# Edge loop of a graph transformer on one core: sums added plainly from a slot read from a table

## The reference

```python
q, k, v = (xn @ Wq + bq), (xn @ Wk + bk), (xn @ Wv + bv)      # xn = layernorm(x), by head
e = edge_attr @ We
alpha = (q[dst] * (k[src] + e)).sum(channels) / sqrt(32)
ea = exp(alpha - segment_max(alpha, dst)[dst])
out = segment_sum((v[src] + e) * ea / (segment_sum(ea, dst)[dst] + 1e-16), dst)
x = x + out + xn @ Ws + bs
x = x + ffn(layernorm(x))       # 8 experts, the best two for each token, 256 -> 512 -> 256
```

## Time and profile before

| | |
|---|---|
| median of 3 runs | 2555.55 us (2554.52 to 2555.57) |
| profiled execution: its time | 2559.0 us |
| its span, first to last instruction | 2557.1 us |
| mean granted TensorE clock | 0.963 of full speed |
| PE busy | 2374.8 us (93%) |
| DVE busy | 2032.8 us (79%) |
| POOL busy | 1809.4 us (71%) |
| ACT busy | 1578.5 us (62%) |

### The profile page before, as it was taken

One profiled execution on the slowest core, in us unless ns is written; L12 is line 12 of the kernel. 1 busy time (PEld: TensorE's weight loads), 2 busy tenths in 40 slices (PEclk: granted clock), 3 DMA queues, 4 the chain that ended last, 5 costly groups with the idle time before them and its releaser, 6 DMA issues. The chain is left out here.

```text
span 2557.1 us, 61957 instructions
## 1 busy us (share of the span) xinstructions
PE 2374.8 (93%) x13310; PEld 1995.0 (78%) x13311; DVE 2032.8 (79%) x5261; ACT 1578.5 (62%) x4373; POOL 1809.4 (71%) x2136
## 2 busy tenths in 40 slices
PE   6998999999999999999999999999995647999998
PEld 3445888888888888888888888888883646999998
DVE  6865999999999999999999999999997773222222
ACT  1122676777777777777777767767774224666665
POOL 4223788888888888888888888878886104666666
PEclk9999999999999999999999999999998558999999
DMA  7326777777787777777777777777772753434443
GB/s 234 127 111 189 234 230 220 227 228 226 224 228 228 222 226 225 223 227 229 227 224 228 228 223 229 226 218 225 228 223 72 234 157 62 70 64 64 69 67 54
DMA packets 337663, 476.35 MB, mean 186 GB/s; under 512 B 61318, under 2 KB 268492, under 8 KB 337052
## 3 DMA queue, kind: packets, MB, share of 16 engines
q0 software_dynamic: 92576, 259.72, 38.4%
q1 hardware_dynamic: 238492, 213.23, 27.7%
q10 hardware_dynamic: 6288, 0.05, 0.1%
HBM read 425.40 MB, written 50.57 MB: 186 GB/s over the span
## 5 line engine op out<-in xcount | busy, mean ns | idle before, releaser
L809 POOL DMA_INDIRECT kv_ring<-vk_table,tab_c x880 | 860.6, 978 | 277.0 <-issue 179.6
L967 PE MATMUL ps_e<-we_sb,aT 128*128 128x256 f32 x3520 | 917.7, 383 | 25.3 <-DVE ve_ke L1055 21.4
L967 PEld LDWEIGHTS ps_e<-we_sb,aT 128*128 128x128 f32 x3520 | 601.1, 191 | 97.8 <-issue 46.0
L1050 DVE TENSOR_TENSOR ve_ke<-kv_ring,ps_e 128x512 f32<-128x512 f32 x880 | 600.5, 682 | 38.4 <-PE ps_e L971 22.0
L819 POOL TENSOR_TENSOR ve_ke<-ve_ke 128x256 f32<-128x256 f32 x880 | 551.3, 630 | 17.7 <-ACT factor L936 4.0
L1020 PE MATMUL ps_u<-ve_ke,sel 128*128 128x264 f32 x1760 | 546.1, 392 | 17.9 <-POOL ve_ke L819 7.6
L971 PE MATMUL ps_e<-q_slots,selT 128*128 x1760 | 517.7, 375 | 0.0
L896 ACT COPY aT<-ps_t 128x256 f32<-128x256 f32 x880 | 325.8, 370 | 301.0 <-PE ps_t L951 265.4
L1126 DVE SCALAR_TENSOR_TENSOR node_slots<-node_slots,same_tile,ps_u 128x264 f32 x880 | 423.4, 481 | 26.2 <-PE ps_u L1020 22.0
L971 PEld LDWEIGHTS ps_e<-q_slots,selT 128*128 128x128 f32 x1760 | 335.0, 190 | 45.8
L1038 DVE TENSOR_REDUCE alpha<-ve_ke 128x8 f32<-128x256 f32 x880 | 363.5, 413 | 1.9
(11 more groups left out here) (249 smaller groups left out, 2648.1 us busy)
## 6 DMA issues: line engine op xcount, KB each, us to landing
a_ring<-in_edge_attr SPq DMA_DIRECT2D x880, 128.0 KB
loc_c<-loc_table SPq DMA_DIRECT2D x220, 128.0 KB
kv_ring<-vk_table,tab_c POOLq DMA_INDIRECT x880
vk_table<-kv_out SPq DMA_DIRECT2D x49, 256.0 KB, 2.0
skip_table<-skip_out SPq DMA_DIRECT2D x49, 128.0 KB, 1.7
skip<-skip_table SPq DMA_DIRECT2D x7, 896.0 KB, 10.2
xn_table<-node_slots SPq DMA_DIRECT2D x7, 896.0 KB, 6.2
out<-node_slots SPq DMA_DIRECT2D x1, 6144.0 KB
```

Of the source, the lines that this page charges most:

```text
L809: g.indirect_dma_start(out=kv_ring[:, i % N_KV, :], out_offset=None, in_=vk_table, in_offset=bass.IndirectOffsetOnAxis(ap=tab_c[:, c % N_T ...
L967: t.matmul(ps_e[i % 2][:, 0:D], aT[i % 2][:, k * P:(k + 1) * P], we_sb[:, k, :], start=(k == 0), stop=(k == KD - 1))
L1050: v.tensor_tensor(ve_ke[:, to:ke + 1:ke - to, 0:D], kv.rearrange("p (t d) -> p t d", t=2), e[:, None, :].to_broadcast([P, 2, D]), ALU.add) ...
```

## The change

- The operation of the addition becomes a plain one of two operands: the sums are read from a slot given by a register. That slot is n itself within a node tile, and a slot of zeros behind the others (number 51) at a node tile's first item. `node_slots` grows by 264 columns for it, and POOL clears them at the start.
- Both numbers of an item stand in one word, source slot times 64 plus node tile, in row 64 of `item_rows`. Three DVE operations in the first stage make it. The word is taken apart with an and and a shift in DVE's registers.
- Four words are loaded at once, behind the key/value addition of a step, four times a chunk; before, it was eight words twice a chunk behind the addition of the sums.
- In the last stage the four buffers `y` lie in the slots of the sums, which are no longer needed, instead of in a place of their own.

```diff
@@ tables @@
+        item_slots = item_rows[64:65, :]
...
-        node_slots = sb("node_slots", [P, NT + 2, SLOT])
+        sums_flat = sb("node_slots", [P, (NT + 2) * SLOT + UW])
+        node_slots = sums_flat[:, 0:(NT + 2) * SLOT].rearrange("p (j w) -> p j w", w=SLOT)
@@ first stage, POOL @@
                 g.memset(node_slots[:, 0, 0:UW], 0.0).then_inc(first_cleared, 1)
+                g.memset(sums_flat[:, (NT + 2) * SLOT:(NT + 2) * SLOT + UW], 0.0).then_inc(first_cleared, 1)
@@ first stage, DVE, behind same_tile @@
+                then(v.scalar_tensor_tensor(out=from_rep[:, :], in0=node_tile_rep[:, :], scalar=float(NT + 2), in1=same_tile[:, :],
+                                            op0=ALU.subtract, op1=ALU.mult))
+                then(v.tensor_scalar(from_rep[:, :], from_rep[:, :], float(NT + 2), float(PACK), ALU.add, ALU.mult))
+                then(v.tensor_tensor(item_slots, from_rep[64:65, :], node_tile_rep[64:65, :], ALU.add))
@@ edge loop, DVE @@
-                def score(c, par, i):
+                def score(c, par, i, meanwhile):
...
                     v.tensor_tensor(ve_ke[:, to:ke + 1:ke - to, 0:D], kv.rearrange("p (t d) -> p t d", t=2),
                                     e[:, None, :].to_broadcast([P, 2, D]), ALU.add).then_inc(s["ve_added"], 1)
+                    meanwhile()
                     if i:
                         reduce(c, par, i - 1)
...
+                AT_ONCE = 4
+                def slots_of(c, i):
+                    some = slice(c * CH + i, c * CH + i + AT_ONCE)
+                    both = nc.values_load_multi_w_load_instructions(
+                        item_slots[0:1, some], engines=[mybir.EngineType.DVE], min_val=0, max_val=(NT + 3) * PACK - 1,
+                        skip_runtime_bounds_check_because="a slot of at most NT + 2 and a tile of at most NT")[1]
+                    return list(both)
...
-                def add(c, i, n, before):
+                def add(c, i, n, source):
                     m = c * CH + i
-                    to, sofar = [sums_flat[:, bass.ds(k * SLOT, UW)] for k in (n, before)]
+                    to, sofar = [sums_flat[:, bass.ds(k * SLOT, UW)] for k in (n, source)]
                     dve.wait_ge(s["summed"], at("summed", m))
                     dve.wait_ge(s["acc_added"], at("acc_added", m - 1))
-                    v.scalar_tensor_tensor(out=to, in0=sofar, scalar=same_tile[:, m:m + 1], in1=ps_u[i % 2][:, 0:UW], op0=ALU.mult, op1=ALU.add
-                                           ).then_inc(s["acc_added"], 1)
+                    v.tensor_tensor(to, sofar, ps_u[i % 2][:, 0:UW], ALU.add).then_inc(s["acc_added"], 1)
...
+                    adds = [(c - b, k) for kind, k, b in steps if kind == "add"]
+                    places = len([1 for kind, k, b in steps if kind == "score"])
+                    def load_next(place):
+                        if adds and place + len(adds) >= places:
+                            cc, k = adds.pop(0)
+                            if k % AT_ONCE == 0:
+                                ahead[:] = slots_of(cc, k)
...
+                            both = ahead.pop(0)
+                            n, source = bounded(both & (PACK - 1), NT), bounded(both >> (PACK.bit_length() - 1), NT + 2)
@@ experts @@
-            y = [sb7(f"y{i}", [P, D]) for i in range(4)]
+            y = [values[:, i, :] for i in range(4)]
```

More of the change, by code:

```diff
@@ L25 @@
 TOP = 2
+PACK = 64
 def ceil_div(a, b):
@@ L111, in gnn_ffn @@
         x_sb = node_slots[:, 1:NT + 1, D:2 * D]
-        sums_flat = node_slots[:, :, :].rearrange("p j w -> p (j w)")
         values, counts = node_slots[:, 0:NT, 0:D], node_slots[:, 0:NT, D:UW]
@@ L166, in gnn_ffn @@
             step_at = sb1("step_at", [NT, 1])
+            from_rep = sb1("from_rep", [P, IT])
             ii_i = sb1("ii_i", [P, IT], I32)
@@ L368, in _ @@
                         resets()
-                pool.wait_ge(first_cleared, 1)
+                pool.wait_ge(first_cleared, 2)
             @block.scalar
@@ L1109, in _ @@
                 last_tile, ahead = [], []
[L1110 to L1119, removed]
@@ L1121, in add, with bounded @@
-                def add(c, i, n, before):
+                AT_ONCE = 4
+                assert NT + 2 < PACK and CH % AT_ONCE == 0
+                def bounded(k, most):
+                    return nc.s_assert_within(k, 0, most, skip_runtime_bounds_check_because="the table holds two slots of this range")
+                def slots_of(c, i):
[4 more added lines that the diff above has]
+                    return list(both)
@@ L1132, in emit @@
                         if kind == "score":
-                            score(c, par, i)
+                            score(c, par, i, lambda: load_next(i))
                         elif kind != "add":
@@ L1136, in emit @@
                         else:
[L1137 to L1140, removed]
+                            if not places:
+                                load_next(CH)
+                            both = ahead.pop(0)
+                            n, source = bounded(both & (PACK - 1), NT), bounded(both >> (PACK.bit_length() - 1), NT + 2)
                             if i == 0:
-                                rescale(c - back, before)
-                            add(c - back, i, n, before)
+                                rescale(c - back, last_tile[0] if last_tile else n)
+                            add(c - back, i, n, source)
                             last_tile[:] = [n]
-                            if i % HALF == HALF - 1 and m_of(c - back, i) + 1 < NCH * CH:
-                                ahead[:] = node_tiles_of((m_of(c - back, i) + 1) // CH, (i // HALF + 1) % 2)
                 over_chunks(dve, emit, what="add", parts={3: "scan", 4: "scan_back", 6: "own", 7: "least", 8: "shift"})
@@ L1621, in put @@
                         out=out, out_offset=bass.IndirectOffsetOnAxis(ap=put_i[:, b:b + 1], axis=0),
-                        in_=y[b % 4][:, :], in_offset=None, bounds_check=N - 1, oob_is_err=False,
+                        in_=y[b % 4], in_offset=None, bounds_check=N - 1, oob_is_err=False,
                         compute_op=ALU.add).then_inc(y_stored[b % 4], 16)
@@ L1737, in weigh @@
                         dve.wait_ge(y_stored[b % 4], 16 * (b // 4))
-                    v.tensor_scalar(y[b % 4][:, :], y_full[b % 2][:, :], gate_of[:, b:b + 1], None, ALU.mult).then_inc(s["y_ready"], 1)
+                    v.tensor_scalar(y[b % 4], y_full[b % 2][:, :], gate_of[:, b:b + 1], None, ALU.mult).then_inc(s["y_ready"], 1)
                 for b in range(NB + 2):
```

## The result

The changed kernel takes 2565.73 us (median of 6 runs, 2563.2 to 2569.36) beside 2554.13 us of the kernel before (6 runs, 2552.51 to 2555.57): a ratio of 1.0044, 95% interval 1.0032 to 1.0056. Forecast were 2510.5 us and a gain; the time lies outside the range and on the other side of no change.

The account below looks back on a forecast made before the run. DVE (30.0 us per chunk) was nearly matched by PE (29.8), which would become the bound: 0.9 us less over 53 chunks, 48 us, less 2.9 for tables, took the 2555.55 us median to 2510.5; range 2490 to 2542.

Parts of the forecast that it names:

- Registers: Register work ahead of each addition in DVE's sequencer: one operation of at most 0.19 us, hidden; bounds 0 to 0.57 us.
- Rival E: DVE's sequencer becomes the bound: 0.57 us of register work per addition, 0.16 exposed, 2627 us in all; chance 0.09.
- Its sign: Forecast wrong towards a sequencer bound if register operations of the addition's line add up to over 0.35 us.
- The sum: Edge loop: DVE's demand falls below PE's 29.8 us, chunk 30.2 us, 0.9 less, 48 us over 53 chunks.
- PE's 0.44 us wait: PE's late weighted matmul after DVE's softmax parts: its wait would shrink to almost nothing.
- The remainder of mutual waiting: Time per chunk that engines still lose waiting for one another: between 0.1 and 1.1 us, taken as 0.4.
- The loads: Two eight-word loads behind the addition expose 0.22 us per chunk; four-word loads behind the key/value addition cost nothing.
- the addition's 62 ns: The plain addition holds DVE 0.062 to 0.07 us less, taken as 0.065 each, 1.04 us per chunk.
- case D: The plain addition is no shorter; only the loads' 0.22 us per chunk is gained, 2547 us; chance 0.04.
- The tables: Three DVE operations ahead of the layer norm: 2.9 us added, nothing hides them, first PE matmul 2.9 us later.
- POOL's pauses: POOL's pauses in the loop, one of 2.99 us and about eight in all, would stay.
- Zero slot: Reading zeros at a tile's first item: same width, no new wait; POOL clears the slot at the start while idle.

Follow-up runs that it names:

- e1: The kernel before with the plain two-operand addition in all 880 places and nothing else of the change: 2530.65 us, ratio 0.9905.
- e10: The kernel before with only the three table operations of the first stage added, their result read by nothing: 2559.93 us, ratio 1.0011.
- e6: The kernel before with only its tile-number loads changed, to four words behind the key/value addition: 2556.98 us, ratio 1.0001.
- e11: The changed kernel with both offsets ready in two table rows, no and or shift, eight four-word loads per chunk: 2535.19 us, 0.9915 to the kernel before.
- e5: The changed kernel, register work meant to move behind the key/value addition, though the operations stayed in place: 2566.15 us, 1.0038 to the kernel before.

## Why the prediction was wrong

The account by single parts, from the ratios: plain addition -24.3 us (e1), tables +2.8 (e10), loads 0 (e6), register work +33 (1.0044 less 0.9915, the changed kernel less e11; their medians lie 30.5 apart). The sum is +11.5 us; measured were 11.2 by the ratio, 11.6 by the medians. The trace gives the same for the register work: 0.63 us per chunk over 53 chunks are 33. The profiled executions differ by only 4.2 (2563.2 - 2559.0): the one before was slower than all its timed runs, the one after was the fastest of its six.

- **Registers: the step that turned the sign.** "I take one operation of at most 0.19, nearest to the present form, which is hidden." There are three, and behind the rescaling it is 0.32 us from the first to the addition where it was 0.10. The upper bound of 0.57 us covered that; the choice did not. The cover was read from one ordinary step, where two other operations fill the engine; the five steps without this cover were not looked at. Rival E had the mechanism at a chance of 0.09, with the price spread evenly over 16 steps from 0.45 us of work on. Measured, the steps with cover cost nothing, and those without cost 0.06 to 0.22 each. Its sign, over 0.35 us of register operations, never showed: the three add up to 0.20 us in the median. That sign asked for their length alone, and where they stand decided too.
- **The sum: the expected gain was too large.** The forecast put 48 us to the addition and the loads, 36 of them to the addition (the loads' 0.22 us per chunk are 12). The plain addition and nothing else gives 24.6. "PE's 0.44 us wait shrinks to almost nothing": it shrank by 0.22, and the three waits by 0.52 of 0.96 saved. The remainder of mutual waiting, taken as 0.4, was a guess between 0.1 and 1.1. The step that failed is the sum by demands. A shorter addition where DVE has caught up with PE only makes it wait sooner: the key/value addition stands over 0.05 us further behind the addition than its least distance in 185 of 850 steps before and in 307 in e1. What it stands behind that least distance adds up to 1.03 us per chunk before and 1.52 in e1. Of 0.96 us saved 0.49 went there, and over the whole loop the chunk became 0.50 shorter. DVE's time without work was forecast at 1.5 us per chunk; it is 1.40 in e1 and 1.74 in the changed kernel. What sets the left-over waiting of the three engines was not worked out by any run.
- **The loads: 12 us forecast, none found.** The 0.11 us behind the loaded step was PE's (e6). The row showed a distance, and I took the sequencer's load as its cause without looking at when PE's matmul of that step ended. The argument that the sequencer runs one operation ahead and not more rested on the same row and falls with it: in the five steps above, what held the sequencer is a wait for DVE's own result. By the Trainium skill, Advanced Engine Details and Errata, "Engine Queue Depths", eight operations fit in the queue, and moving the loads would bring nothing. e6 agrees in the time (1.0001), but the load lay in a wait for PE, so how deep the queue is no run here shows.
- **Right:** the addition's 62 ns (59 measured; 0.40 to 0.34 us start to start), which rules out case D. The tier table of the Trainium skill (VectorE: DVE Perf Modes, "The perf-mode tier table") has the 1x mode alone for a plain fp32 addition with a PSUM operand, and no row for the three-operand form; taken as the whole price of these operations, it would have given nothing. e1 does not agree, with 24.6 us. The tables: 2.9 forecast, 2.8 measured, though within 0.3 to 5.1; PE's first matmul came 3.0 us later. POOL's pauses stayed, one at every 110th gather in both kernels. Zero slot, waits and output buffers show no cost of their own, since e11 has them all and lies where its other parts put it.

**What stays open.** Whether the and and the shift would be free if they were placed behind the key/value addition: e5 did not move them. And how the 33 us divide over the five steps: their costs were read from the trace, but none was changed alone.

## What to carry to other kernels

Where several engines are nearly full, as here, a saving counts only as far as it shortens a wait of the engine that sets the pace: find these waits, start to start, and follow each back, instead of subtracting demands. Look for the steps in which the operation ahead waits for the engine's own last result: there an address worked out in registers lay open, 0.06 to 0.22 us each time, and the finished offset in a table took that away. And before a distance is put down to one cause, look at several of its kind: a constant one comes from the engine itself, another engine's result may end inside it.

## What was unexpected

- A wait for an engine's own result hides from the trace twice: the operation ahead shows no idle time worth noting, and the idle time behind it was put down to PE, whose sum had been ready long before. The 0.47 and 0.69 us, nearly the same in every chunk, gave it away.
- An and and a shift make three operations out of one: fused ones of 57 to 116 ns with a plain one of 40 between them (e11 with plain offsets: one of 69).
- A load of four words takes DVE's sequencer 343 ns and one of eight 597, but the eight shorter ones per chunk in e11 cost nothing that can be seen beside e1 (30.22 and 30.21 us per chunk).
